# Switched attention: the pair products of two tiles in one matmul, in odd slots

## The chip, the cores and the metric

The kernel runs on one core of a Trainium2 chip. The metric is the time of one execution of the whole program in microseconds (us), taken on the device; lower is better. The figures for the kernel before come from three runs and from one profiled execution.

## The reference

The reference is a decoder of four blocks over x of 128 x 64 x 128 floats. Each block adds an attention and a feed-forward part. The change touches only the last part, a switched attention over 8 heads with 8 experts each, of which 2 are chosen for each token and head:

```python
gate_v = _get_sel_gate(x, sel_v_w, rs)      # sigmoid of the logits, top 2 of 8, normalised
gate_o = _get_sel_gate(x, sel_o_w, rs)
q = jnp.einsum('bsd,hpd->bhsp', x, q_w.reshape(H, P, D))
k = jnp.einsum('bsd,hpd->bhsp', x, k_w.reshape(H, P, D))
xv = jnp.einsum('bsd,hedp->bshep', x, v_w.reshape(H, E, D, P))
v = jnp.einsum('bshep,bshe->bhsp', xv, gate_v)
att = jax.nn.softmax(jnp.einsum('bhqp,bhkp->bhqk', q, k) * SCALE, axis=-1)
ctx = jnp.einsum('bhqk,bhkp->bqhp', att, v)
weighted = ctx[:, :, :, None, :] * gate_o[..., None]
out = jnp.einsum('bshep,hepd->bsd', weighted, o_w.reshape(H, E, P, D))
```

Its input is the layer norm of x, and its result is added to x times a gate.

## The kernel before

The last part is `switch_attention` (L1731 on). The other parts come before it and end at about 1211 us of the profiled span. Work is cut into 64 tiles of 128 tokens (two sequences of 64). `straight` (L36) writes each engine's program: for slot t = 0, 1, 2 ... it goes through that engine's list of stages `(lag, step)` and calls `step(t - lag)`. So a slot holds steps of several tiles, the order inside it is the order of the list, and every engine works through its own list strictly in order. Semaphores (`q[...]`) join the engines.

What a slot holds on each engine:

- TensorE: 16 units (`unit`, L2202 on), v0 to v7 of one tile and o0 to o7 of the tile before it. A unit is six 128x512 matmuls at L2221 on numbers split in a high and a low part: three fill bank `ps_a` (experts 4 to 7), three fill bank `ps_d` (experts 0 to 3). There are two banks of each, so unit n waits until unit n-2 has been read. Between the units stand small fp32 products: `turn_x` (L2229), `turn_probs` (L2236, two halves), `logits` (L2243), `pair_keys` (L2254), `scores` (L2278) and `context` (L2267).
- `pair_keys` multiplies the turned x of a tile with a 128x128 matrix per head, W["pair"] (key weights times query weights, made once), and so gives u; `scores` multiplies u with x. It is done in two halves of four heads, in banks `ps_w[0]` and `ps_w[1]`; `context` writes the same two banks.
- ScalarE scales `ps_a` with the gates (L1962, four instructions for a unit), and copies x, u (`keep_u`, L1993), the turned probabilities and the context out of PSUM; `exp_logits` (L1985) starts the routing of a tile.
- VectorE mixes `ps_d` into the sums (L2117, four instructions for a unit). Between these halves of units stand the 20 steps R0 to R19 of `route` (L2126 to L2147), which need `exp_logits`. They begin after the first half of v3, and a table, `between`, gives each its place.
- GpSimd adds the parts up: `add_v` (L1889, L1894) for each v unit, `add_o` for each o unit, `finish` for the output.

`context` of a tile stands on TensorE behind o1 and waits for v of all eight heads:

```python
wait_alone(pe, (q["v"], SH * i + SH), (q["p_kept"], i + 1), (q["uT"], 2 * upto))
```

The lags before are 1 for turn_x, pair_keys, logits, scores and routing, 2 for the v units, the turned probabilities and context, and 3 for the o units. The weights are loaded and split in a high and a low part once: V in slot 1, O in slots 2 and 3 (16 halves, between the v units' steps on ScalarE, L2023, and on VectorE, L2063).

Of the kernel before, what the change touches and what calls it, by code (L numbers as in the profile page):

```python
# [1730 lines left out]
def switch_attention(k, A, C, x_in, out):  # L1731
# [6 lines left out]
    with k.scope():  # L1738
# [31 lines left out]
        place = k.sb("sw_place", [P, 2 * SH, SE])  # L1770
# [3 lines left out]
        r = {n: k.sb("sw_r_" + n, G) for n in ("plus", "p", "eq1", "w1", "sel1", "p2", "eq2", "w2", "sel2", "sel")}  # L1774
# [47 lines left out]

        with nc.Block() as block:
            @block.sync
            def _(sp):
# [5 lines left out]
                sp.dma_start(place[:], A["c_place"].rearrange("p (g e) -> p g e", e=SE)).then_inc(q["place"], 16)  # L1831
# [203 lines left out]
            def _(dve):  # L2035
# [85 lines left out]
                def route(n):  # L2121


                    def step(i, s, rd):
                        ops = [
                            lambda: dve.tensor_scalar(r["plus"][:], decays[:], 1.0, None, ALU.add),  # L2126
                            lambda: dve.reciprocal(r["p"][:], r["plus"][:]),
                            lambda: dve.tensor_reduce(rm["m1"][:], r["p"][:], AX.X, ALU.max),
                            lambda: dve.tensor_tensor(r["eq1"][:], r["p"][:], wide(rm["m1"][:]), ALU.is_equal),
                            lambda: dve.tensor_tensor(r["w1"][:], r["eq1"][:], place[:], ALU.mult),  # L2130
                            lambda: dve.tensor_reduce(rm["w1"][:], r["w1"][:], AX.X, ALU.max),
                            lambda: dve.tensor_tensor(r["sel1"][:], r["w1"][:], wide(rm["w1"][:]), ALU.is_equal),
                            lambda: dve.scalar_tensor_tensor(out=r["p2"][:], in0=r["sel1"][:], scalar=-2.0, in1=r["p"][:],
                                                             op0=ALU.mult, op1=ALU.add),
                            lambda: dve.tensor_reduce(rm["m2"][:], r["p2"][:], AX.X, ALU.max),
                            lambda: dve.tensor_tensor(r["eq2"][:], r["p2"][:], wide(rm["m2"][:]), ALU.is_equal),
                            lambda: dve.tensor_tensor(r["w2"][:], r["eq2"][:], place[:], ALU.mult),
                            lambda: dve.tensor_reduce(rm["w2"][:], r["w2"][:], AX.X, ALU.max),
                            lambda: dve.tensor_tensor(r["sel2"][:], r["w2"][:], wide(rm["w2"][:]), ALU.is_equal),
                            lambda: dve.tensor_tensor(r["sel"][:], r["sel1"][:], r["sel2"][:], ALU.add),  # L2140
                            lambda: dve.tensor_tensor(chosen[:, s], r["p"][:], r["sel"][:], ALU.mult),
# [245 lines left out]
```

## Time and profile before

| | us |
|---|---|
| median of three runs | 3170.46 |
| lowest, highest | 3169.66, 3173.8 |
| profiled execution, its own time | 3168.74 |
| its span in the trace | 3167.0 |
| TensorE busy | 2907.0 (92%) |
| VectorE busy | 2780.7 (88%) |
| ScalarE busy | 2341.8 (74%) |
| GpSimd busy | 2322.8 (73%) |

The profiled execution is 1.7 us under the median, and its span is 1.7 us under its own time. Busy shares are means over all parts. In the timeline a row gives the start, the time from the first start to the last end, the engine, the line, and what it writes from what; times in square brackets are idle time before it and what ended it. Matmuls overlap in the pipeline, so the distance from start to start tells what one costs the engine, not its length. An fp32 matmul leaves two records, so "x8" at L2254 is four matmuls.

### The profile page before, as it was taken

To read this page: it belongs to the slowest core of one execution; us is meant where nothing else is said; L and a number is where in the kernel's file an instruction comes from. 1 tells how busy PE (TensorE), PEld (TensorE's weight loads), DVE (VectorE), ACT (ScalarE), POOL (GpSimd) and SP (SyncE) were. 2 spreads that over 40 slices of the span, in tenths; PEclk is the share of its full clock that TensorE was granted. 3 is DMA by queue.
4 is the path that set the end of the run, shared out by engine and by line. 5 is a ranking of instruction groups with operands and counts; after the bars stand their busy time and mean duration, and the time that the engine had idled before them with its cause. 6 is when DMAs were issued, how large, how long until landed. Compare 5 with 4: busy or idle time off the path is not lost.

```text
span 3167.0 us, 78218 instructions
## 1 busy us (share of the span) xinstructions
PE 2907.0 (92%) x24620; PEld 2176.0 (69%) x24620; DVE 2780.7 (88%) x9085; ACT 2341.8 (74%) x7546; POOL 2322.8 (73%) x3112
## 2 busy tenths in 40 slices
PE   7489992897689996999999999999999999999998
PEld 7257762675357774677777777777777777777776
DVE  6789997899989986888888888898898898898897
ACT  4866668888976665777777777777777777777776
POOL 2799994666876662677777777777777777777777
PEclk8589995898789997999999999999999999999999
DMA  4000000220000004100000000000000000000000
GB/s 131 8 2 2 2 2 18 68 75 13 1 6 16 16 16 109 30 9 8 7 9 8 7 9 8 7 9 8 7 9 8 8 9 8 7 9 8 7 8 6
DMA packets 114508, 55.31 MB, mean 17 GB/s; under 512 B 18352, under 2 KB 113712, under 8 KB 114096
## 3 DMA queue, kind: packets, MB, share of 16 engines
q1 hardware_dynamic: 114096, 50.30, 5.8%
q8 instruction: 200, 3.28, 0.4%
q14 instruction: 212, 1.74, 0.2%
HBM read 41.81 MB, written 8.45 MB: 16 GB/s over the span
## 4 chain that ended last, share of the span: by engine, by line
PE 59%; DVE 1%; ACT 1%; POOL 1%; DMA 0%; issue 0%; SPq 0%; POOLq 0%; ACTq 0%; DVEq 0%
PE ps_sw_a L2221 24%; PE ps_sw_d L2221 22%; PE ps_sw_w L2267 4%; PE ps_sw_w L2254 3%; PE ps_sw_s L2236 2%; PE ps_sw_s L2278 2%; PE ps_sw_m L2243 1%; ACT sw_scaled L1962 0%; DVE sw_v_part L2117 0%; PE ps_sw_m L2229 0%; DMA sw_v<-in_L_ffn_v_w 0%; POOL sw_v_pair L1889 0%; DVE sw_v_low L2056 0%; DVE sw_o_low L2063 0%; ACT sw_v_high L2017 0%
## 5 line engine op out<-in xcount | busy, mean ns | idle before, releaser
L1962 ACT ACTIVATE sw_scaled<-ps_sw_a,sw_gate_o 128x128 f32<-128x128 f32 x2048 | 620.3, 447 | 254.1 <-PE ps_sw_a L2221 247.0
L1962 ACT ACTIVATE sw_scaled<-ps_sw_a,sw_gate_v 128x128 f32<-128x128 f32 x2048 | 597.3, 448 | 196.2 <-PE ps_sw_a L2221 194.4
L2117 DVE SCALAR_TENSOR_TENSOR sw_o_part<-ps_sw_d,sw_gate_o,sw_o_part 128x128 f32<-128x128 f32 x1920 | 555.6, 339 | 63.1 <-PE ps_sw_d L2221 60.5
L1889 POOL TENSOR_TENSOR sw_v_pair<-sw_v_part,sw_scaled 128x256 f32<-128x256 f32 x512 | 381.9, 746 | 157.0 <-DVE sw_v_part L2117 91.6
L2117 DVE SCALAR_TENSOR_TENSOR sw_v_part<-ps_sw_d,sw_gate_v,sw_scaled 128x128 f32<-128x128 f32 x1024 | 303.9, 337 | 126.1 <-PE ps_sw_d L2221 107.1
L1915 POOL TENSOR_TENSOR sw_o_rest<-sw_o_rest,sw_scaled 128x256 f32<-128x256 f32 x384 | 285.4, 743 | 158.0 <-ACT sw_scaled L1962 120.7
L2117 DVE SCALAR_TENSOR_TENSOR sw_v_part<-ps_sw_d,sw_gate_v,sw_v_part 128x128 f32<-128x128 f32 x1024 | 304.8, 339 | 0.0
L1918 POOL TENSOR_TENSOR sw_o_rest<-sw_o_rest,sw_scaled 128x256 f32<-128x256 f32 x384 | 282.6, 736 | 30.1
L1894 POOL TENSOR_TENSOR sw_v<-sw_v_pair 128x128 f32<-128x128 f32 x512 | 244.6, 478 | 40.1
L1014 POOL TENSOR_TENSOR at_key_wide<-at_keyT,c_half_heads 128x1024 f32<-128x1024 f32 x128 | 242.6, 1895 | 4.6 <-ACT at_keyT L1112 4.6
L2221 PE MATMUL ps_sw_a<-sw_v_high,sw_xT_high 128*128 128x512 f32 x512 | 234.5, 458 | 8.2 <-DVE sw_v_low L2056 8.2
L2221 PE MATMUL ps_sw_a<-sw_o_high,sw_ctx_high 128*128 128x512 f32 x512 | 215.7, 421 | 0.2 <-ACT sw_scaled L1962 0.2
L2221 PE MATMUL ps_sw_d<-sw_v_high,sw_xT_high 128*128 128x512 f32 x512 | 207.6, 405 | 0.3 <-DVE sw_v_part L2117 0.3
L2221 PE MATMUL ps_sw_d<-sw_o_high,sw_ctx_high 128*128 128x512 f32 x512 | 202.1, 395 | 1.2 <-DVE sw_v_part L2117 1.2
L2221 PE MATMUL ps_sw_d<-sw_o_low,sw_ctx_high 128*128 128x512 f32 x512 | 202.7, 396 | 0.0
L2221 PE MATMUL ps_sw_a<-sw_o_high,sw_ctx_low 128*128 128x512 f32 x512 | 202.7, 396 | 0.0
L2221 PE MATMUL ps_sw_a<-sw_v_high,sw_xT_low 128*128 128x512 f32 x512 | 202.5, 396 | 0.0
L2221 PE MATMUL ps_sw_a<-sw_v_low,sw_xT_high 128*128 128x512 f32 x512 | 202.2, 395 | 0.0
L2221 PE MATMUL ps_sw_d<-sw_o_high,sw_ctx_low 128*128 128x512 f32 x512 | 202.1, 395 | 0.0
L2221 PE MATMUL ps_sw_a<-sw_o_low,sw_ctx_high 128*128 128x512 f32 x512 | 202.1, 395 | 0.0
L2221 PE MATMUL ps_sw_d<-sw_v_high,sw_xT_low 128*128 128x512 f32 x512 | 201.8, 394 | 0.0
L2221 PE MATMUL ps_sw_d<-sw_v_low,sw_xT_high 128*128 128x512 f32 x512 | 200.7, 392 | 0.0
(337 smaller groups left out, 8511.3 us busy)
## 6 DMA issues: line engine op xcount, KB each, us to landing
re_values<-in_ctx SPq DMA_DIRECT2D x128, 64.0 KB, 2.4
l_ctx<-in_ctx SPq DMA_DIRECT2D x16, 256.0 KB, 4.5
x<-in_x SPq DMA_DIRECT2D x16, 256.0 KB, 4.6
re_ctx<-in_ctx SPq DMA_DIRECT2D x16, 256.0 KB, 3.1
scratch_x<-x SPq DMA_DIRECT2D x64, 64.0 KB, 1.5
sw_x<-scratch_x SPq DMA_DIRECT2D x64, 64.0 KB, 1.9
sw_x_res<-scratch_x SPq DMA_DIRECT2D x64, 64.0 KB, 1.8
out<-sw_y SPq DMA_DIRECT2D x64, 64.0 KB, 1.5
```

Source lines behind the costliest of these rows:

```text
L1014: pool.tensor_tensor(key_wide[:, s], keyT[:, s].unsqueeze(1).broadcast_to([P, HALF, P]), C["half_heads"][:].unsqueeze(2).broadcast_to([P, ...
L1889: pool.tensor_tensor(v_pair[:, h % 2], v_part[:, h], scaled[:, h % 4, 2:4], ALU.add)\
L1894: pool.tensor_tensor(v[:, h], v_pair[:, h % 2, 0], v_pair[:, h % 2, 1], ALU.add).then_inc(q["v"], 1)
L1915: pool.tensor_tensor(o_rest[:, 0:2], o_rest[:, 0:2], scaled[:, h % 4, 0:2], ALU.add)\
L1918: pool.tensor_tensor(o_rest[:, 2:4], o_rest[:, 2:4], scaled[:, h % 4, 2:4], ALU.add)\
L1962: act.activation(scaled[:, h % 4, e], ps_a[h % 2][:, e], ACT.Copy, scale=gates[:, s, h, HALF_E + e:HALF_E + e + 1]).then_inc(a_scaled[kind ...
L2117: dve.scalar_tensor_tensor(out=acc[:, e % 2], in0=ps_d[h % 2][:, e], scalar=gates[:, s, h, e:e + 1], in1=before, op0=ALU.mult, op1=ALU.add ...
L2221: m = pe.matmul(bank, lhs[a], w[b][:, h, experts], start=c == 0, stop=c == 2)
L2236: m = pe.matmul(ps_s[t, h], probs[t, s, h], C["ident"][t, t], start=True, stop=True)
L2254: m = pe.matmul(ps_w[n][:, h * P:(h + 1) * P], W["pair"][:, 4 * n + h], xT[:, s], start=True, stop=True)
L2267: m = pe.matmul(ps_w[b][:, h * S:(h + 1) * S], v[t, h], probs_T[t, h], start=True, stop=True)
L2278: m = pe.matmul(ps_s[t], xT[:, s, t], uT[:, :, t], start=True, stop=True)
```

## The change

Pair products are made for two tiles at once. x of four tiles is kept (`xT` has four places), u for two (`uT` [P, SH, 2, P]). `pair_keys` runs only for even tiles and multiplies each pair matrix with the 256 columns of x of tiles i and i+1. Its eight matmuls for a pair of tiles (before: sixteen of 128 columns) stand in two blocks of four: the first directly behind the first half of the turned probabilities, the second between v4 and v5. With the new lag of 3 they all fall in odd slots. The lags are now 1 for turn_x, 3 for pair_keys, logits, scores, routing and the rounded x, 4 for v, turned probabilities and context, 5 for o, 6 for the store. The preparation of the weights keeps its lags 1 to 3. ScalarE's rounded x is made from `xT` in SBUF, behind the second unit, and a pair has four `keep_u` copies as before, now all in one slot, two of them ahead of `exp_logits`. To make room the routing works in place: three tiles in the place of ten, and one row of `place` read by all groups.

```diff
-        xT = k.sb("sw_xT", [P, 2, P])
+        xT = k.sb("sw_xT", [P, 4, P])
...
-        uT = k.sb("sw_uT", [P, SH, P])
+        uT = k.sb("sw_uT", [P, SH, 2, P])
...
-        r = {n: k.sb("sw_r_" + n, G) for n in ("plus", "p", "eq1", "w1", "sel1", "p2", "eq2", "w2", "sel2", "sel")}
+        r = {n: k.sb("sw_r_" + n, G) for n in ("equal", "sel", "p2")}
...
+        def of_pair(step):
+            def at(i, s, rd):
+                if i % 2 == 0:
+                    step(i, s, rd)
+            return at
...
-                    act.activation(xT[:, s], ps_m[:, 0], ACT.Copy).then_inc(q["xT"], 1)
-                    act.activation(xT_high[:, s], ps_m[:, 0], ACT.Copy).then_inc(q["xT_high"], 1)
+                    act.activation(xT_high[:, s], xT[:, i % 4], ACT.Copy).then_inc(q["xT_high"], 1)
...
-                        act.activation(uT[:, 4 * n:4 * n + 4], ps_w[n].rearrange("p (h t) -> p h t", h=4), ACT.Copy)\
-                            .then_inc(q["uT"], 1)
-                    return step
+                        act.activation(uT[:, 2 * n:2 * n + 2], ps_w[n % 2].rearrange("p (h c t) -> p h c t", h=2, c=2),
+                                       ACT.Copy).then_inc(q["uT"], 1)
+                    return of_pair(step)
...
-                stages = vs[:2] + [(1, keep_x)] + vs[2:4] + [(1, exp_logits), (2, keep_probs)] + vs[4:6]
-                stages += [(1, keep_u(0)), vs[6], (1, keep_u(1)), vs[7]] + os[:3] + [(2, keep_ctx(0)), os[3], exps[0]]
...
+                stages = vs[:2] + [(1, keep_x), (3, round_x), vs[2], (3, keep_u(0)), vs[3], (3, keep_u(1)), (3, exp_logits), (4, keep_probs)]
+                stages += [vs[4], vs[5], (3, keep_u(2)), vs[6], (3, keep_u(3)), vs[7]] + os[:3]
...
+                            both = xT[:, i % 4:i % 4 + 2].rearrange("p c t -> p (c t)")
+                            for h in range(2):
+                                m = pe.matmul(ps_w[n % 2][:, 2 * h * P:2 * (h + 1) * P], W["pair"][:, 2 * n + h], both,
+                                              start=True, stop=True)
+                            m.then_inc(q["u"], 1)
+                    return of_pair(step)
...
-                    wait_alone(pe, (q["v"], SH * i + SH), (q["p_kept"], i + 1), (q["uT"], 2 * upto))
-                    if isinstance(i, int) and i == TILES - 1:
+                    wait_alone(pe, (q["v"], SH * i + SH), (q["p_kept"], i + 1))
+                    if i % 2 and i < TILES - 1:
+                        pe.wait_ge(q["uT"], 2 * (i + 3))
+                    elif i:
                         pe.wait_ge(q["ctx_low"], 2 * i)
...
-                stages = vs[:2] + [(1, turn_x), turns[0], vs[2], turns[1], (1, logits), vs[3], vs[4], (1, pair_keys(0))]
-                stages += [vs[5], (1, pair_keys(1)), vs[6], vs[7], os[0], (1, scores), os[1], (2, context)]
-                stages += os[2:]
+                turns = [(4, lambda i, s, rd, lo=lo: turn_probs(i, s, rd, lo)) for lo in (0, 4)]
+                stages = vs[:2] + [(1, turn_x), turns[0], (3, pair_keys(0)), vs[2], turns[1], (3, logits), vs[3], vs[4], (3, pair_keys(2))]
+                stages += vs[5:] + [os[0], (3, scores), os[1], (4, context)] + os[2:]
```

TensorE from the turned x behind v1 to the first product of v2, before, in every slot:

```order
L2229 MATMUL ps_sw_m<-c_ident,sw_xhat 128x128
L2236 MATMUL ps_sw_s<-c_ident,sw_probs 64x64 x8
L2221 MATMUL ps_sw_a<-sw_v_high,sw_xT_high 128x512
L2221 MATMUL ps_sw_a<-sw_v_low,sw_xT_high 128x512
L2221 MATMUL ps_sw_a<-sw_v_high,sw_xT_low 128x512
```

The same place now, in an odd slot:

```order
L2243 MATMUL ps_sw_m<-c_ident,sw_xhat 128x128
L2250 MATMUL ps_sw_s<-c_ident,sw_probs 64x64 x8
L2272 MATMUL ps_sw_w<-sw_xT,sw_pair 128x256 x4
L2233 MATMUL ps_sw_a<-sw_v_high,sw_xT_high 128x512
L2233 MATMUL ps_sw_a<-sw_v_low,sw_xT_high 128x512
L2233 MATMUL ps_sw_a<-sw_v_high,sw_xT_low 128x512
```

Four matmuls of 256 columns have come in ahead of v2; an even slot has none there. A second place, TensorE from the end of v4 on, before, in every slot (`sw_w<-sw_xT,sw_pair` is pair_keys):

```order
L2221 MATMUL ps_sw_d<-sw_v_high,sw_xT_low 128x512
L2254 MATMUL ps_sw_w<-sw_xT,sw_pair 128x128 x4
L2221 MATMUL ps_sw_a<-sw_v_high,sw_xT_high 128x512
L2221 MATMUL ps_sw_a<-sw_v_low,sw_xT_high 128x512
L2221 MATMUL ps_sw_a<-sw_v_high,sw_xT_low 128x512
L2221 MATMUL ps_sw_d<-sw_v_high,sw_xT_high 128x512
L2221 MATMUL ps_sw_d<-sw_v_low,sw_xT_high 128x512
L2221 MATMUL ps_sw_d<-sw_v_high,sw_xT_low 128x512
L2254 MATMUL ps_sw_w<-sw_xT,sw_pair 128x128 x4
```

Now, in an odd slot, one block is left there, of 256 columns, and none stands between v5 and v6; in an even slot both are gone. ScalarE around `exp_logits` (`sw_exp`), before, in every slot:

```order
L1962 ACTIVATE sw_scaled<-ps_sw_a,sw_gate_v 128x128 x8
L1985 ACTIVATE sw_exp<-ps_sw_m 128x128
L1979 ACTIVATE sw_probs_T<-ps_sw_s 128x512
L1962 ACTIVATE sw_scaled<-ps_sw_a,sw_gate_v 128x128 x8
L1993 ACTIVATE sw_uT<-ps_sw_w 128x512
```

And now, in an odd slot, from v2 on:

```order
L1968 ACTIVATE sw_scaled<-ps_sw_a,sw_gate_v 128x128 x4
L2004 ACTIVATE sw_uT<-ps_sw_w 128x512
L1968 ACTIVATE sw_scaled<-ps_sw_a,sw_gate_v 128x128 x4
L2004 ACTIVATE sw_uT<-ps_sw_w 128x512
L1996 ACTIVATE sw_exp<-ps_sw_m 128x128
L1990 ACTIVATE sw_probs_T<-ps_sw_s 128x512
L1968 ACTIVATE sw_scaled<-ps_sw_a,sw_gate_v 128x128 x8
L2004 ACTIVATE sw_uT<-ps_sw_w 128x512
```

Two copies of u have moved ahead of `exp_logits`, one of them between the scaling of v3 and it. VectorE's order inside a slot is as before.

## Rows read from the trace of the kernel before

**Rows 1.** The page's first part: busy time, share of the span, instructions.
```profile
PE 2907.0 (92%) x24620; PEld 2176.0 (69%) x24620; DVE 2780.7 (88%) x9085; ACT 2341.8 (74%) x7546; POOL 2322.8 (73%) x3112
```
**Rows 2.** Busy time by stretches: span, PE, PEld, DVE, ACT, POOL, clock, DMA, GB/s.
```profile
2000.00:2200.00 200.00, 199.90 (x1225) 153.21 (x1223) 180.26 (x646) 152.13 (x595) 151.64 (x235) 1.00 0.03 8
```
**Rows 3.** Timeline of TensorE, context of two tiles, 29 slots apart.
```profile
1329.52 2.00 PE L2267 MATMUL ps_sw_w<-sw_probs_T,sw_v 64*128 64x64 f32 x32
...
2188.78 2.00 PE L2267 MATMUL ps_sw_w<-sw_probs_T,sw_v 64*128 64x64 f32 x32
```
**Rows 4.** Timeline of TensorE in one slot, from v0 to context.
```profile
2051.24 0.47 PE L2221 MATMUL ps_sw_a<-sw_v_high,sw_xT_high 128*128 128x512 f32 x1
...
2058.76 0.39 PE L2221 MATMUL ps_sw_d<-sw_v_high,sw_xT_low 128*128 128x512 f32 x1
...
2060.15 0.39 PE L2221 MATMUL ps_sw_d<-sw_v_high,sw_xT_low 128*128 128x512 f32 x1
2060.38 1.05 PE L2254 MATMUL ps_sw_w<-sw_xT,sw_pair 128*128 128x128 f32 x8
2061.18 0.48 PE L2221 MATMUL ps_sw_a<-sw_v_high,sw_xT_high 128*128 128x512 f32 x1
2061.49 0.40 PE L2221 MATMUL ps_sw_a<-sw_v_low,sw_xT_high 128*128 128x512 f32 x1
...
2067.77 1.08 PE L2278 MATMUL ps_sw_s<-sw_uT,sw_xT 128*64 128x512 f32 x4
2068.78 0.50 PE L2221 MATMUL ps_sw_a<-sw_o_high,sw_ctx_high 128*128 128x512 f32 x1
...
2070.37 2.00 PE L2267 MATMUL ps_sw_w<-sw_probs_T,sw_v 64*128 64x64 f32 x32
```
**Rows 5.** Timeline of VectorE in the same slot.
```profile
2059.23 0.61 DVE L2117 SCALAR_TENSOR_TENSOR sw_v_part<-ps_sw_d,sw_gate_v,sw_scaled 128x128 f32<-128x128 f32 x2 [1.17 <-PE ps_sw_d L2221]
2059.84 0.23 DVE L2126 TENSOR_SCALAR sw_r_plus<-sw_exp 128x128 f32<-128x128 f32 x1
...
2064.47 0.81 DVE L2132 TENSOR_TENSOR sw_r_sel<-sw_r_w,sw_m_w 128x128 f32<-128x128 f32 x1
...
2066.75 0.81 DVE L2136 TENSOR_TENSOR sw_r_eq<-sw_r_p,sw_m_m 128x128 f32<-128x128 f32 x1
...
2068.20 0.60 DVE L2117 SCALAR_TENSOR_TENSOR sw_v_part<-ps_sw_d,sw_gate_v,sw_v_part 128x128 f32<-128x128 f32 x2
...
2074.01 0.61 DVE L2117 SCALAR_TENSOR_TENSOR sw_o_part<-ps_sw_d,sw_gate_o,sw_o_part 128x128 f32<-128x128 f32 x2 [0.89 <-PE ps_sw_d L2221]
```
**Rows 6.** Timeline of GpSimd in the same slot: parts of v6 and v7.
```profile
2066.66 0.74 POOL L1889 TENSOR_TENSOR sw_v_pair<-sw_v_part,sw_scaled 128x256 f32<-128x256 f32 x1 [0.99 <-ACT sw_scaled L1962]
...
2068.94 0.74 POOL L1889 TENSOR_TENSOR sw_v_pair<-sw_v_part,sw_scaled 128x256 f32<-128x256 f32 x1 [1.00 <-DVE sw_v_part L2117]
2069.76 0.46 POOL L1894 TENSOR_TENSOR sw_v<-sw_v_pair 128x128 f32<-128x128 f32 x1
```
**Rows 7.** Timeline of ScalarE in the same slot, behind the scaling of v3.
```profile
2059.51 0.30 ACT L1985 ACTIVATE sw_exp<-ps_sw_m 128x128 f32<-128x128 f32 x1
2059.67 0.63 ACT L1979 ACTIVATE sw_probs_T<-ps_sw_s 128x512 f32<-128x512 f32 x1
2060.15 1.18 ACT L1962 ACTIVATE sw_scaled<-ps_sw_a,sw_gate_v 128x128 f32<-128x128 f32 x4
```
**Rows 8.** Start of the part: ScalarE's V halves, VectorE's O half, the first context.
```profile
1236.00 2.04 ACT L2017 ACTIVATE sw_v_high<-sw_v_part 128x1024 fp32r<-128x1024 f32 x2
...
1251.71 0.68 DVE L2063 TENSOR_TENSOR sw_o_low<-sw_o_part,sw_o_high 128x512 fp32r<-128x512 f32 x1
...
1272.22 3.68 PE L2267 MATMUL ps_sw_w<-sw_probs_T,sw_v 64*128 64x64 f32 x32 [5.86 <-POOL sw_v L1894]
```
**Rows 9.** DMA issues from 1200 to 1320 us: count, KB, us to landing.
```profile
sw_o_part<-in_L_ffn_o_w SPq DMA_DIRECT2D x4, 256.0 KB, 3.8
```
**Rows 10.** VectorE at the start of the part, GpSimd idle.
```profile
1229.53 0.29 DVE L2132 TENSOR_TENSOR sw_r_sel<-sw_r_w,sw_m_w 128x128 f32<-128x128 f32 x1
```

More of the change, by code:

```diff
@@ L1830, in _ @@
                 sp.dma_start(route_scale[:], on_all(A["L3_ffn_route_scale"], 1)).then_inc(prep["small"], 16)
[L1831 removed]
+                sp.dma_start(place[:], A["c_place"][:, 0:SE]).then_inc(q["place"], 16)
                 def tile_in(dst, i):
@@ L2124, in step @@
                     def step(i, s, rd):
+                        p = decays
                         ops = [
[L2126 to L2130, printed above, removed]
@@ L2131, in step @@
-                            lambda: dve.tensor_reduce(rm["w1"][:], r["w1"][:], AX.X, ALU.max),
-                            lambda: dve.tensor_tensor(r["sel1"][:], r["w1"][:], wide(rm["w1"][:]), ALU.is_equal),
-                            lambda: dve.scalar_tensor_tensor(out=r["p2"][:], in0=r["sel1"][:], scalar=-2.0, in1=r["p"][:],
+                            lambda: dve.tensor_scalar(p[:], decays[:], 1.0, None, ALU.add),
+                            lambda: dve.reciprocal(p[:], p[:]),
+                            lambda: dve.tensor_reduce(rm["m1"][:], p[:], AX.X, ALU.max),
@@ new lines, in step @@
+                            lambda: dve.tensor_tensor(r["equal"][:], p[:], wide(rm["m1"][:]), ALU.is_equal),
+                            lambda: dve.tensor_tensor(r["equal"][:], r["equal"][:], place[:].unsqueeze(1).broadcast_to(G), ALU.mult),
+                            lambda: dve.tensor_reduce(rm["w1"][:], r["equal"][:], AX.X, ALU.max),
+                            lambda: dve.tensor_tensor(r["sel"][:], r["equal"][:], wide(rm["w1"][:]), ALU.is_equal),
+                            lambda: dve.scalar_tensor_tensor(out=r["p2"][:], in0=r["sel"][:], scalar=-2.0, in1=p[:],
@@ L2140, in step @@
-                            lambda: dve.tensor_tensor(r["sel"][:], r["sel1"][:], r["sel2"][:], ALU.add),
-                            lambda: dve.tensor_tensor(chosen[:, s], r["p"][:], r["sel"][:], ALU.mult),
+                            lambda: dve.tensor_tensor(r["equal"][:], r["p2"][:], wide(rm["m2"][:]), ALU.is_equal),
+                            lambda: dve.tensor_tensor(r["equal"][:], r["equal"][:], place[:].unsqueeze(1).broadcast_to(G), ALU.mult),
+                            lambda: dve.tensor_reduce(rm["w2"][:], r["equal"][:], AX.X, ALU.max),
@@ L2241, in logits, with pair_keys @@
                         pe.wait_ge(prep["kept"], 1)
-                    pe.wait_ge(q["xT_high"], i + 1)
-                    pe.matmul(ps_m[:, 1], xT[:, s], W["sel"][:], start=True, stop=True).then_inc(q["logits"], 1)
-                def pair_keys(n):
+                    pe.wait_ge(q["xT"], min(i + 3, TILES))
+                    pe.matmul(ps_m[:, 1], xT[:, i % 4], W["sel"][:], start=True, stop=True).then_inc(q["logits"], 1)
+                def pair_keys(lo):
                     def step(i, s, rd):
-                        if i == 0:
-                            pe.wait_ge(prep["kept"], 2 + n)
-                        elif not first(i, 2):
-                            pe.wait_ge(q["ctx_low"], 2 * (i - 2) + n + 1)
-                        else:
-                            pe.wait_ge(q["uT"], 1 + n)
-                        for h in range(4):
-                            m = pe.matmul(ps_w[n][:, h * P:(h + 1) * P], W["pair"][:, 4 * n + h], xT[:, s],
-                                          start=True, stop=True)
-                        m.then_inc(q["u"], 1)
-                    return step
+                        if lo == 0:
+                            pe.wait_ge(q["xT"], i + 2)
+                        for n in (lo, lo + 1):
+                            if n >= 2:
+                                pe.wait_ge(q["uT"], 2 * i + n - 1)
+                            elif i == 0:
+                                pe.wait_ge(prep["kept"], 3)
+                            else:
+                                pe.wait_ge(q["ctx_low"], 2 * (i - 2) + n + 1)
+                            both = xT[:, i % 4:i % 4 + 2].rearrange("p c t -> p (c t)")
[4 more added lines that the diff above has]
+                    return of_pair(step)
@@ L2271, in scores @@
                 def scores(i, s, rd):
-                    waits = [(q["uT"], 2 * i + 2)]
+                    waits = [(q["uT"], 4 * (i // 2) + 4)]
                     if not first(i, 1):
@@ L2277, in scores @@
                         t = slice(b * S, (b + 1) * S)
-                        m = pe.matmul(ps_s[t], xT[:, s, t], uT[:, :, t], start=True, stop=True)
+                        m = pe.matmul(ps_s[t], xT[:, i % 4, t], uT[:, :, s, t], start=True, stop=True)
                     m.then_inc(q["scores"], 1)
```

58 lines of the change are left out of this document (32 added, 26 removed).

## Prediction

> **What bounds the kernel now.** I read the busy shares first: TensorE 92% over the whole, VectorE 88% [rows 1]. In a steady stretch of the last part TensorE is busy without a gap (199.90 of 200 us) at a granted clock of 1.00, and VectorE stands at 180.26, 90% [rows 2]. That looks like a kernel bound by TensorE alone. Then the regularity: 29 slots take 2188.78 - 1329.52 = 859.26 us, 29.63 us each [rows 3]. So one slot can stand for all, and what is left is to ask how much slack the other engines have in it.
>
> For that I follow one slot from engine to engine. TensorE's last product of v3 starts at 2058.76 and lasts 0.39 [rows 4]. VectorE has waited 1.17 us for it and starts on v3 at 2059.23 [rows 5]. From there it has no idle time until behind v7: its next wait, 0.89 us, is the one at 2074.01. It ends v7 at about 2068.8. GpSimd takes v7 at 2068.94 and ends at 2069.76 + 0.46 = 2070.22 [rows 6]. TensorE starts context at 2070.37 [rows 4]. So there are two ways from v3 to context, TensorE's own products (11.6 us from 2058.76) and the way over VectorE's v3 to v7 and GpSimd, and they end within 0.15 us of each other. Some of that is the time from a signal to a start; I take the slack as 0.10. **This is the fact that decides**: from v3 to context TensorE can get faster by 0.1 us and no more, whatever is taken out of it. From context round to v3 of the next slot it is the other way round: VectorE waits for TensorE (0.89 us at the first o unit behind context, 1.17 at v3), so each us added to TensorE there is added to the slot.
>
> **The change part by part.**
>
> *Pair products, price.* A block of four (eight records) of 128 columns goes from 2060.38 to 2061.18, 0.80 us, and the product behind it takes 0.31 to the next start where 0.23 is normal (2060.15 to 2060.38) [rows 4]: 0.88 in all, 3.52 for a pair of tiles. The new block has eight records of 256 columns. Below, a record can't be cheaper than one of half the columns: 0.80 / 8 = 0.10, 0.88 for the block. Above, it can't be dearer than one of 512 columns, 1.01 / 4 = 0.25 at the scores, 2.0 for the block. Half of a 512-column record is 0.125, barely over the 0.10 that a 128-column record with its weights takes, so I take 0.12, with 0.04 for a weight load that nothing hides: 1.0 us a block, 2.0 for a pair. TensorE saves 1.5 us per pair of tiles.
>
> At the scores an fp32 matmul of 512 columns takes 0.505 us (1.01 for two) [rows 4]. The Trainium skill, "FP8 and Floating Point Precision", section "TensorE Precision Notes", says that true fp32 takes four passes through the array; at 2.4 GHz (granted clock 1.00) that would be 0.85 us for 512 columns, an estimate from that page, and a new block would be 1.7 us, which would make the sum 21 us longer. The trace disagrees, and its number is used.
>
> *Where they stand.* Both old blocks stood between v4 and v6, on the stretch with 0.1 us of slack. An even slot loses both, 1.76 us, and can use 0.1: TensorE will wait ahead of o0's second bank and at context instead. Even slot: 29.63 - 0.10 = 29.53. An odd slot has one block between v4 and v5 (TensorE's way there is 11.6 - 1.76 + 1.0 = 10.8 us, still shorter than the other), and one ahead of v2, on the stretch where VectorE waits for TensorE: +1.0 in full.
>
> *Copies ahead of exp_logits.* exp_logits starts at 2059.51 and ends at 2059.81, and VectorE's R0 starts at 2059.84, in the middle of its gapless run [rows 5, 7]. In an odd slot a copy of 128x512 now stands between the scaling of v3 and exp_logits. Such a copy holds ScalarE for 2060.15 - 2059.67 = 0.48 us [rows 7]. R0 and all behind it start 0.48 later: +0.48. The bounds are 0 (if ScalarE has it behind it in time) and 0.6. The first of these copies, ahead of v3, is hidden: there TensorE's product of v3 is what ScalarE waits for, as VectorE does. The copies behind v5 and v6 stand as before. Keeping x before rounding it, the rounding from SBUF and the longer lags add nothing to either way in a steady slot: what they feed is wanted a slot later.
>
> *Routing in place.* The same 20 operations with the same shapes, in the same places on VectorE, each waiting for the one before as now: 0, bounds -0.2 and +0.2 per slot.
>
> *Odd slot*: 29.53 + 1.0 + 0.48 = 31.01. A pair of slots is 60.54 against 59.26: +1.28.
>
> *The two more slots at the start.* V's preparation was queued on ScalarE behind tile 0's softmax and starts at 1236.00 [rows 8]; now tile 0's softmax is in slot 3, and V can start up to 10 us earlier. But all 16 halves of O now stand ahead of v0 of tile 0, where half of them lay between its units. A round of four buffers is a landing of 3.8 us [rows 9], a rounding of about 0.65, a subtraction of 0.68 [rows 8] and an issue, 5.5 us, so four rounds take 22: V ready at about 1239, the first four halves half loaded by then, O at about 1257, the softmax at 1259. A slot takes 2070.37 - 2051.24 = 19.1 us from v0 to context [rows 4], so the first context comes at 1278 (now 1272.22), the second, behind 2 us of context, in an odd slot, at 1300.5, the third 29.5 later, at 1330. It is at 1329.52 now [rows 3]. Fill: +0.5, bounds -8 and +12. The end has the same steps, shifted by two slots: 0.
>
> *Sum.* Odd slots from 7 to 65 are 30: 30 x 1.28 = 38.4, and 0.5: +39. On the profiled execution's 3168.74 us that is 3207.6. The median of the runs is 1.7 higher than that execution, so I forecast **3208 us**, between the two.
>
> **The rivals.**
>
> *Slower, but by more.* A record of 256 columns costs near 0.25, so a block 2.0. Only the block ahead of v2 counts, the other has 1.2 us of room: +1.0 per pair, 3238. Against: half of the 512-column record. Chance 0.08.
>
> *Nothing that can be told.* A single VectorE wait of 0.5 us goes in every slot and the late exp_logits is hidden: a pair is 29.03 + 30.03 = 59.06, -6 us. Within 0.2% (6 us, about what a measurement of this kernel can tell from no change): 0.05.
>
> *Faster, TensorE alone decides.* If the other way had slack that I don't see, the whole 1.52 us per pair would be gained, 31 times, 47 us: 3122. For it: the gapless TensorE [rows 2]. It decides from 1.7 us of slack per slot on; I read 0.1. Chance 0.08.
>
> *Faster, VectorE's run shortens.* Two of its operations take 0.81 us (at 2064.47 and 2066.75), and the second starts within 0.1 us of GpSimd's part of v6 at 2066.66 and ends with it [rows 5, 6]; the same operation with GpSimd idle took 0.29 [rows 10]. If the moved work parts them, the run is 1.0 us shorter, a slot 28.53, an odd one 30.01, a pair 58.54: -0.72, 3147. It decides from 0.65 us per slot on. Against: GpSimd starts there because VectorE has just ended the unit, so the two stay tied in every slot. Chance 0.09. The Trainium skill, "SBUF — State Buffer", section "SBUF: two separate sides", gives this mechanism: the two share a port pair that one of them holds for a whole instruction. The trace agrees.
>
> **How the numbers follow.** My forecast, with its own range 3190 to 3222 (fill -8 to +12, exp_logits from 0 to 0.6), has 0.70; the rivals 0.08, 0.05, 0.08, 0.09. Slower by over 0.2%: 0.78; same 0.05; faster 0.17. The range leaves out the two faster cases (0.17) and the far end of the dear block: 3178 to 3230.
>
> **What would show it.** Right: context to context alternates, near 29.5 and 31.0; in TensorE's timeline the product ahead of o0's second bank and context wait 1.5 us in even slots, ended by VectorE and GpSimd; the block ahead of v2 takes about 1.0; VectorE's wait for v2 or v3 is 1 us longer in odd slots, and a wait of 0.5 us for ScalarE appears ahead of R0; VectorE's time at L2117 is as before. Wrong: slots that alternate near 28 and 30 with TensorE still gapless (TensorE alone), operations of 0.81 fallen to 0.3 (the shorter run), or a first context later than 1290 (fill).

## The result and the profile after

The changed kernel takes 3256.1 us (median of four runs, 3251.69 to 3257.53), the kernel before 3171.94 in the same session. The ratio is 1.0263, 95% interval 1.0246 to 1.0281: 84 us slower. The forecast had the sign and the alternating slots, but only 39 us more, and its range ended at 3230. The profiled execution took 3255.74, with a span of 3254.0 against 3167.0: 87.0 us to explain.

First the page's first part of the changed kernel (busy time, share of the span, instructions), then its busy time by stretches from 2000 to 2200 us (span, PE, PEld, DVE, ACT, POOL, clock, DMA, GB/s).

```profile
PE 2935.1 (90%) x24095; PEld 2145.2 (66%) x24108; DVE 2785.9 (86%) x9085; ACT 2345.3 (72%) x7546; POOL 2314.1 (71%) x3112
```

```profile
2000.00:2200.00 200.00, 195.73 (x1140) 144.21 (x1138) 172.72 (x618) 148.16 (x582) 149.48 (x232) 1.00 0.03 8
```

Every engine is as busy in total as before, within 1% [rows 1], and all are idler in the steady stretch [rows 2]: TensorE has lost 4 us of 200 to waits where it had no gap, at the same granted clock. TensorE issues 512 records fewer (24108, as the weight loads count; 13 matmul records are missing from this trace) and is busy 28 us longer. Now TensorE's timeline, context of tiles 2 and 62 and of three tiles between them:

```profile
1341.61 2.00 PE L2288 MATMUL ps_sw_w<-sw_probs_T,sw_v 64*128 64x64 f32 x32
...
2021.07 2.00 PE L2288 MATMUL ps_sw_w<-sw_probs_T,sw_v 64*128 64x64 f32 x32
...
2053.24 2.00 PE L2288 MATMUL ps_sw_w<-sw_probs_T,sw_v 64*128 64x64 f32 x32
...
2082.80 2.00 PE L2288 MATMUL ps_sw_w<-sw_probs_T,sw_v 64*128 64x64 f32 x32
...
3194.02 2.00 PE L2288 MATMUL ps_sw_w<-sw_probs_T,sw_v 64*128 64x64 f32 x32
```

Slots alternate: 32.17 us (odd) and 29.56 (even), where each took 29.63 [rows 3]. From tile 2 to tile 62 it is 1852.41 us; before, with the contexts at 1329.52 and 3107.06, 1777.54: 74.9 more. From the last of these to the end it is 59.98 against 59.94. The rest, 12.1, lies ahead of tile 2's context: 2.2 of it before the part begins (VectorE's first instruction of the part is at 1216.67 against 1214.49; the change touches nothing there, and over the profiled executions of this document that start scatters from 1211.63 to 1218.85), 9.9 in the part's start.

The two blocks of one odd slot, TensorE's timeline (start, length, engine, line, output and inputs):

```profile
2034.82 0.68 PE L2250 MATMUL ps_sw_s<-c_ident,sw_probs 64*64 64x64 f32 x16
2035.43 1.99 PE L2272 MATMUL ps_sw_w<-sw_xT,sw_pair 128*128 128x256 f32 x8
2037.08 0.58 PE L2233 MATMUL ps_sw_a<-sw_v_high,sw_xT_high 128*128 128x512 f32 x1
2037.49 0.39 PE L2233 MATMUL ps_sw_a<-sw_v_low,sw_xT_high 128*128 128x512 f32 x1
...
2042.43 1.89 PE L2272 MATMUL ps_sw_w<-sw_xT,sw_pair 128*128 128x256 f32 x8
2043.97 0.58 PE L2233 MATMUL ps_sw_a<-sw_v_high,sw_xT_high 128*128 128x512 f32 x1
2044.38 0.40 PE L2233 MATMUL ps_sw_a<-sw_v_low,sw_xT_high 128*128 128x512 f32 x1
```

From start to start the first block costs 2037.08 - 2035.43 = 1.65, and the product behind it 0.41 where 0.23 is normal: 1.83 us. The second costs 1.54 and 0.18, 1.72. Together 3.55 for a pair of tiles, against 3.52 for the four old blocks [rows 4]. **Joining the products saved TensorE nothing**: 256 columns cost twice what 128 do. The forecast had 1.0.

VectorE in the same slot; in square brackets the idle time ahead of a row and what ended it:

```profile
2038.88 0.61 DVE L2128 SCALAR_TENSOR_TENSOR sw_v_part<-ps_sw_d,sw_gate_v,sw_scaled 128x128 f32<-128x128 f32 x2 [2.04 <-PE ps_sw_d L2233]
...
2041.30 0.61 DVE L2128 SCALAR_TENSOR_TENSOR sw_v_part<-ps_sw_d,sw_gate_v,sw_scaled 128x128 f32<-128x128 f32 x2 [0.72 <-PE ps_sw_d L2233]
2042.40 0.23 DVE L2138 TENSOR_SCALAR sw_exp<-sw_exp 128x128 f32<-128x128 f32 x1 [0.49 <-ACT sw_exp L1996]
...
2045.78 0.61 DVE L2128 SCALAR_TENSOR_TENSOR sw_v_part<-ps_sw_d,sw_gate_v,sw_scaled 128x128 f32<-128x128 f32 x2 [0.44 <-PE ps_sw_d L2233]
...
2047.46 0.81 DVE L2144 TENSOR_TENSOR sw_r_sel<-sw_r_equal,sw_m_w 128x128 f32<-128x128 f32 x1
```

The first row is v2: VectorE waits 2.04 for the block ahead of it, where it waited 0.58 before. The wait of 0.49 for ScalarE ahead of R0 is there, as forecast. The fourth row is not in the forecast: VectorE waits again at v5, for TensorE, whose second block stands ahead of v5. v5 starts 4.48 us behind v3, and before it was 3.68 (2062.91, below, against 2059.23 [rows 5]). The 0.81-us operation is unchanged, so the rival of VectorE's shorter run is out. The same two rows, v2 and v5, before:

```profile
2056.80 0.61 DVE L2117 SCALAR_TENSOR_TENSOR sw_v_part<-ps_sw_d,sw_gate_v,sw_scaled 128x128 f32<-128x128 f32 x2 [0.58 <-PE ps_sw_d L2221]
...
2062.91 0.60 DVE L2117 SCALAR_TENSOR_TENSOR sw_v_part<-ps_sw_d,sw_gate_v,sw_scaled 128x128 f32<-128x128 f32 x2
```

Last TensorE's waits in an odd and the next even slot, at o0's second bank, and between them GpSimd's last v of the odd slot. It ends at 2052.73 + 0.46 = 2053.19, and context starts at 2053.24:

```profile
2049.55 0.50 PE L2233 MATMUL ps_sw_d<-sw_o_high,sw_ctx_high 128*128 128x512 f32 x1 [0.43 <-DVE sw_v_part L2128]
```

```profile
2052.73 0.46 POOL L1900 TENSOR_TENSOR sw_v<-sw_v_pair 128x128 f32<-128x128 f32 x1
```

```profile
2079.10 0.50 PE L2233 MATMUL ps_sw_d<-sw_o_high,sw_ctx_high 128*128 128x512 f32 x1 [0.59 <-DVE sw_v_part L2128]
```

So in both kinds of slot the way over VectorE and GpSimd now sets the end of the stretch from v3 to context. An odd slot is 29.56 + 1.83 ahead of v2 + 0.80 at v5 = 32.19, against 32.17 seen.

### The profile page after: what moved, and what is told of

It is laid out like the page before. It is cut to its first block, busy times and chain, and to the rows that moved or that the text cites. A ratio compares the mean times of both kernels' runs of the same rounds, so it can differ in the third digit from the quotient of the medians.

```text
span 3254.0 us, 77178 instructions
## 1 busy us (share of the span) xinstructions
PE 2935.1 (90%) x24095; PEld 2145.2 (66%) x24108; DVE 2785.9 (86%) x9085; ACT 2345.3 (72%) x7546; POOL 2314.1 (71%) x3112
## 4 chain that ended last, share of the span: by engine, by line
PE 47%; DVE 7%; ACT 4%; issue 3%; POOL 1%; DMA 1%; SPq 0%; DVEq 0%; ACTq 0%; POOLq 0%
PE ps_sw_a L2233 18%; PE ps_sw_d L2233 16%; DVE sw_v_part L2128 5%; PE ps_sw_w L2288 4%; ACT sw_scaled L1968 4%; PE ps_sw_w L2272 4%; PE ps_sw_s L2250 2%; PE ps_sw_s L2299 1%; PE ps_sw_m L2257 1%; DVE sw_r_equal L2142 0%; DVE sw_r_p L2145 0%; DMA sw_v<-in_L_ffn_v_w 0%; POOL sw_v_pair L1895 0%; DVE sw_m_w L2143 0%; PE ps_sw_m L2243 0%
## 5 line engine op out<-in xcount | busy, mean ns | idle before, releaser
L2233 PE MATMUL ps_sw_d<-sw_o_high,sw_ctx_high 128*128 128x512 f32 x512 | 208.8, 408 | 32.2 <-DVE sw_v_part L2128 32.2
```

The lines of the kernel that those rows point to most:

```text
L2233: m = pe.matmul(bank, lhs[a], w[b][:, h, experts], start=c == 0, stop=c == 2)
```

## The experiments

The theory behind them: taking TensorE work off the stretch from v3 to context gains 0.1 us of a slot at most, and work added anywhere costs what it takes. So the cost is the price of a block, weighed by its place. What was open was the price, why the row of the scores had misled, and what the late exponential and the start of the part are worth.

**Both blocks behind v4.**

```diff
-stages = vs[:2] + [(1, turn_x), turns[0], (3, pair_keys(0)), vs[2], turns[1], (3, logits), vs[3], vs[4], (3, pair_keys(2))]
-stages += vs[5:] + [os[0], (3, scores), os[1], (4, context)] + os[2:]
+stages = vs[:2] + [(1, turn_x), turns[0], vs[2], turns[1], (3, logits), vs[3], vs[4], (3, pair_keys(0)), vs[5], vs[6], (3, pair_keys(2))]
+stages += vs[7:] + [os[0], (3, scores), os[1], (4, context)] + os[2:]
...
```

ScalarE's list changes with it (not shown): all four copies of u stand behind v4, and `exp_logits` directly behind v3.

> The changed kernel (3256.1) with both blocks of pair products between v4 and v7 of odd slots, and ScalarE's copies behind them, so that exp_logits stands directly behind the scaling of v3 again. Theory A (from v3 to context TensorE has room for the two old blocks, 1.76 us, in every slot and no more; outside that stretch a block costs its whole price; a block of 256 columns is 1.83): even slots stay at 29.5; in odd slots TensorE's way from v3 to context is 11.6 - 1.76 + 3.66 = 13.5, 1.9 more than the other way, and nothing stands ahead of v2: 31.4 to 31.5. A pair 61.0 against 61.73, 20 us less, about 3236. Theory B (the dear part of the change is only the block ahead of v2 and the late exp_logits): odd 29.6, a pair 59.2, about 3180. Theory C (the place is of no account, the longer lags or the routing cost the time): within 6 us of 3256.

Measured: 3227.3 us (ratio to before 1.0174, 1.0159 to 1.0189), 29 less than the changed kernel. The contexts of an odd slot:

```profile
2009.71 2.00 PE L2288 MATMUL ps_sw_w<-sw_probs_T,sw_v 64*128 64x64 f32 x32
...
2040.95 2.00 PE L2288 MATMUL ps_sw_w<-sw_probs_T,sw_v 64*128 64x64 f32 x32
```

31.24, expected 31.4 to 31.5; even slots 29.51. The time was expected at 3236. A block behind v4 costs 1.72 and the two 3.44, 1.68 more than before, and 29.63 + 1.68 = 31.31. Theory A stands, with the price read a little too high, and theories B and C fall.

**Only 64 stationary columns.**

```diff
-m = pe.matmul(ps_w[n % 2][:, 2 * h * P:2 * (h + 1) * P], W["pair"][:, 2 * n + h], both,
+m = pe.matmul(ps_w[n % 2][0:S, 2 * h * P:2 * (h + 1) * P], W["pair"][:, 2 * n + h, 0:S], both,
```

> The changed kernel (3256.1) with only 64 of the 128 columns of each pair matrix as the stationary operand: the matmuls still have 256 moving columns, all copies and places are as in the changed kernel, and half of the key components is left out of the scores. Theory A (an fp32 product with 128 stationary columns takes twice the passes of one with 64, which is why the scores, with 64, told me too low a price): a record falls from 0.207 to about 0.11 us and a block from 1.83 to 0.9 to 1.0. The block ahead of v2 gives 0.9 back in every odd slot, and the one behind v4 whatever v5's wait for TensorE is, 0.3: odd 31.0, about 3256 - 36 = 3220 (3215 to 3228). Theory B (the price goes by moving columns alone): no record changes, within 6 us of 3256. Theory C (the slot waits for GpSimd and VectorE whatever TensorE does ahead of v2): records get shorter and the time stays at 3256.

Measured: 3266.9 (ratio 1.0300, 1.0285 to 1.0316), slower than the changed kernel. A block with its start and the product behind it:

```profile
2042.12 1.94 PE L2272 MATMUL ps_sw_w<-sw_xT,sw_pair 128*64 128x256 f32 x8
2043.99 0.50 PE L2233 MATMUL ps_sw_a<-sw_v_high,sw_xT_high 128*128 128x512 f32 x1
```

The block takes 1.87 us. **Theory A, as put here, is wrong**: fewer stationary columns make an fp32 product no cheaper.

**Two halves side by side.** What is left that sets the scores apart is their output: one of their two products writes partitions 0 to 63, the other 64 to 127.

```diff
-m = pe.matmul(ps_w[n % 2][:, 2 * h * P:2 * (h + 1) * P], W["pair"][:, 2 * n + h], both,
+m = pe.matmul(ps_w[n % 2][h * S:(h + 1) * S, 2 * h * P:2 * (h + 1) * P], W["pair"][:, 2 * n + h, 0:S], both,
```

> The narrow stationary operand alone made nothing cheaper (a block of four 64-column products still took 1.87 us, and the time was 3266.9), so theory A as put for it has fallen. New theory D: what makes the scores cheap (1.01 us for two products of 512 columns) is that the two write different halves of the partitions, 0 to 63 and 64 to 127, and so run side by side in two halves of TensorE's columns; each takes its full four passes. This run is the changed kernel with 64 of the 128 columns of each pair matrix, as in the narrow run, but the two products of one bank write different halves of the partitions (half of the key components is left out). D: a block falls from 1.87 to 0.9 to 1.0; that is the price that my prediction had, so it also tests the rest of its sum: odd slots 31.0, even 29.53, fill +12, 3171.9 + 38 + 12 = 3222 (3210 to 3228). Rival E (the shape of the moving operand, 512 columns in steps, is what makes the scores cheap): the block stays at 1.87 and the time at 3267.

```profile
2015.91 1.08 PE L2272 MATMUL ps_sw_w<-sw_xT,sw_pair 128*64 128x256 f32 x8
2016.93 0.50 PE L2233 MATMUL ps_sw_a<-sw_v_high,sw_xT_high 128*128 128x512 f32 x1
```

Measured: 3213.2 (ratio 1.0138, 1.0124 to 1.0152). The same eight records with the same operand shapes cost 1.02 instead of 1.87 by their place in the output alone. D stands and E falls. The contexts of an odd and an even slot:

```profile
2001.58 2.00 PE L2288 MATMUL ps_sw_w<-sw_probs_T,sw_v 64*128 64x64 f32 x32
...
2032.51 2.00 PE L2288 MATMUL ps_sw_w<-sw_probs_T,sw_v 64*128 64x64 f32 x32
...
2062.01 2.00 PE L2288 MATMUL ps_sw_w<-sw_probs_T,sw_v 64*128 64x64 f32 x32
```

With a block near the forecast's price, odd slots are 30.93 and even ones 29.50; the forecast had 31.01 and 29.53. Where the price is right, the rest of its sum for a steady slot holds.

**The scores written to one half.** The converse, on the kernel before. It leaves out the scores of the second sequence of each tile; four matmuls at the start (not shown) fill the bank once.

```diff
-m = pe.matmul(ps_s[t], xT[:, s, t], uT[:, :, t], start=True, stop=True)
+m = pe.matmul(ps_s[0:S], xT[:, s, t], uT[:, :, t], start=True, stop=True)
```

> The kernel before with both products of the scores written to partitions 0 to 63 (the scores of the second sequence of a tile are left out, those of the first are overwritten; four matmuls at the start fill the bank once). Theory D (side by side in two halves of the columns): written to one half they run one after the other, and scores take 1.75 to 1.9 us instead of 1.01. As the stretch from v3 to context has 0.1 of room, each slot gets 0.65 to 0.8 longer, 64 of them 42 to 51: 3214 to 3223. Rival E (an fp32 product of 512 columns takes 0.5 us by itself): the scores stay at 1.01 and the time at 3172.

```profile
2026.93 1.93 PE L2278 MATMUL ps_sw_s<-sw_uT,sw_xT 128*64 128x512 f32 x4
2028.79 0.50 PE L2221 MATMUL ps_sw_a<-sw_o_high,sw_ctx_high 128*128 128x512 f32 x1
...
2030.38 2.00 PE L2267 MATMUL ps_sw_w<-sw_probs_T,sw_v 64*128 64x64 f32 x32
...
2060.88 2.00 PE L2267 MATMUL ps_sw_w<-sw_probs_T,sw_v 64*128 64x64 f32 x32
```

Measured: 3220.0 (ratio 1.0157, 1.0143 to 1.0171). The scores take 1.86 us instead of 1.01 [rows 4], so one fp32 product of 512 columns takes 0.93, not the 0.505 that the forecast took. The slot is 30.50, 0.87 longer: on this stretch TensorE's added work has no room at all.

**exp_logits ahead of the second copy of u**, with the dear and with the cheap block (the same edit to the changed kernel and to the one with two halves):

```diff
-[..., (3, keep_u(0)), vs[3], (3, keep_u(1)), (3, exp_logits), (4, keep_probs)]
+[..., (3, keep_u(0)), vs[3], (3, exp_logits), (3, keep_u(1)), (4, keep_probs)]
```

> The changed kernel (3256.1) with exp_logits ahead of the second copy of u. Theory A (VectorE waits 0.49 for exp_logits at R0, but behind it v5 waits 0.44 for TensorE's second block, so the late exponential is hidden under that wait): the wait at R0 goes, the wait of v5's mixing grows from 0.44 to 0.9, no difference over 3 us. Theory B (the late exponential costs its 0.48 in every odd slot, as the prediction had it): 30 x 0.48 = 14 us less, 3242.

> The run with the pair products in two halves (half of the key components is left out), with exp_logits ahead of the second copy of u. With the dear block, exp_logits first gave 0.15 us in an odd slot (32.17 to 32.01). If D is right, TensorE's second block no longer delays v5, and the late exponential costs its whole 0.48: 30 x 0.48 = 14 us less than the run with exp_logits behind the copy, about 3207. Rival: it is hidden elsewhere, and the gain is 5 us or less, as with the dear block.

Measured: 3254.4 (ratio 1.0260, 1.0245 to 1.0275), odd slots 32.02, and v5's wait is 0.79: theory A. With the cheap block 3217.5 (ratio 1.0153, 1.0139 to 1.0167), odd slots 31.10 where they were 30.93: 4 us slower, and neither expectation holds. The intervals of the two times overlap, but from tile 2 to tile 62 the second profile is 6.2 us longer. VectorE's rows for v3 and v5 of an odd slot, first with two halves, then with the exponential first as well:

```profile
2021.09 0.61 DVE L2128 SCALAR_TENSOR_TENSOR sw_v_part<-ps_sw_d,sw_gate_v,sw_scaled 128x128 f32<-128x128 f32 x2 [0.76 <-PE ps_sw_d L2233]
2022.18 0.23 DVE L2138 TENSOR_SCALAR sw_exp<-sw_exp 128x128 f32<-128x128 f32 x1 [0.49 <-ACT sw_exp L1996]
...
2025.08 0.61 DVE L2128 SCALAR_TENSOR_TENSOR sw_v_part<-ps_sw_d,sw_gate_v,sw_scaled 128x128 f32<-128x128 f32 x2
2025.60 0.36 DVE L2142 TENSOR_TENSOR sw_r_equal<-sw_r_equal,sw_place 128x128 f32<-128x128 f32 x1
```

```profile
2022.71 0.61 DVE L2128 SCALAR_TENSOR_TENSOR sw_v_part<-ps_sw_d,sw_gate_v,sw_scaled 128x128 f32<-128x128 f32 x2 [0.73 <-PE ps_sw_d L2233]
...
2026.69 0.61 DVE L2128 SCALAR_TENSOR_TENSOR sw_v_part<-ps_sw_d,sw_gate_v,sw_scaled 128x128 f32<-128x128 f32 x2 [0.29 <-PE ps_sw_d L2233]
2027.22 0.56 DVE L2142 TENSOR_TENSOR sw_r_equal<-sw_r_equal,sw_place 128x128 f32<-128x128 f32 x1
```

With the exponential late there is a wait of 0.49 ahead of R0 and none at v5; with it early there is none at R0 and 0.29 at v5. v5 starts 3.99 and 3.98 behind v3 either way. So the late exponential and TensorE's block ahead of v5 are two ways to the same place, and the longer counts, not the sum. Behind v5 the second run is 0.2 longer at L2142 (0.56 against 0.36), which over 30 odd slots is 6 us. GpSimd's rows beside the two, first with two halves, then with the exponential first as well:

```profile
2025.07 0.74 POOL L1895 TENSOR_TENSOR sw_v_pair<-sw_v_part,sw_scaled 128x256 f32<-128x256 f32 x1 [0.73 <-ACT sw_scaled L1968]
```

```profile
2027.17 0.46 POOL L1900 TENSOR_TENSOR sw_v<-sw_v_pair 128x128 f32<-128x128 f32 x1
```

They end at 2025.81 and 2027.63, and VectorE's operation ends 0.15 us behind each (2025.96 and 2027.78), as its 0.81-us operation ends 0.16 behind GpSimd's [rows 5, 6]. So the length of L2142 goes with where GpSimd's work falls. That is read from the rows; no run moved GpSimd's work alone.

**Both: two halves, and both blocks behind v4**: the kernel of the first experiment with the edit of the third. Two of its added lines:

```diff
+stages = vs[:2] + [(1, turn_x), turns[0], vs[2], turns[1], (3, logits), vs[3], vs[4], (3, pair_keys(0)), vs[5], vs[6], (3, pair_keys(2))]
...
+m = pe.matmul(ps_w[n % 2][h * S:(h + 1) * S, 2 * h * P:2 * (h + 1) * P], W["pair"][:, 2 * n + h, 0:S], both,
```

> Both ideas together: the block at the price that my prediction had (two products side by side in two halves of the columns, 1.01 us; half of the key components is left out) and both blocks between v4 and v7 with exp_logits directly behind the scaling of v3. Theory (price times place): TensorE's way from v3 to context in odd slots is 11.6 - 1.76 + 2.03 = 11.9, 0.3 more than before and 0.4 over the other way; odd slots 29.9 to 30.1, even 29.5, a pair 59.4 to 59.6 against 59.26, 30 pairs +4 to +10, and the start +7 to +10: 3183 to 3190. Rival (joining the products for two tiles costs something beyond TensorE's time, by the copies of u or the waits of pairs): odd slots stay over 30.5 and the time over 3200.

Measured: 3194.5 (ratio 1.0074, 1.0057 to 1.0091), over the expectation's 3190. TensorE around the first block, and the contexts at the two ends of that odd slot:

```profile
2057.49 2.00 PE L2288 MATMUL ps_sw_w<-sw_probs_T,sw_v 64*128 64x64 f32 x32
...
2076.89 0.39 PE L2233 MATMUL ps_sw_d<-sw_v_high,sw_xT_low 128*128 128x512 f32 x1
2077.21 1.08 PE L2272 MATMUL ps_sw_w<-sw_xT,sw_pair 128*64 128x256 f32 x8
2078.23 0.50 PE L2233 MATMUL ps_sw_a<-sw_v_high,sw_xT_high 128*128 128x512 f32 x1
...
2087.81 2.00 PE L2288 MATMUL ps_sw_w<-sw_probs_T,sw_v 64*128 64x64 f32 x32
```

The product ahead of a block of this kind takes 0.32 to the next start and not 0.23, and the one behind it 0.34: a block is 1.02 + 0.09 + 0.11 = 1.22, two 2.44, 0.68 more than before. Odd slots are 2087.81 - 2057.49 = 30.32, 0.69 more. My 1.01 had left the neighbours out. In this profiled execution the rest is the start of the part, 7.2 longer than before up to tile 2's context.

**The lags alone**: the kernel before with the new lags, four places of x, two of u, x rounded from SBUF and the routing in place, but with products of 128 columns per tile at the old places:

```diff
-vs, os = ([(lag, unit(kind, h)) for h in range(SH)] for kind, lag in (("v", 2), ("o", 3)))
+vs, os = ([(lag, unit(kind, h)) for h in range(SH)] for kind, lag in (("v", 4), ("o", 5)))
...
-m = pe.matmul(ps_w[n][:, h * P:(h + 1) * P], W["pair"][:, 4 * n + h], xT[:, s],
+m = pe.matmul(ps_w[n][:, h * P:(h + 1) * P], W["pair"][:, 4 * n + h], xT[:, i % 4],
```

> The kernel before (3171.9) with all of the change but the joined products: lags 1/3/4/5/6, four places of x, two of u, rounded x from SBUF behind the second unit, routing in place; the pair products stay per tile, 128 columns, at the old places in every slot. Theory A (the steady slot pays only for the blocks, the two more slots at the start cost 12 us): slots of 29.63, first context at 1285, 12 us more, about 3184 (3178 to 3190). Theory B (the longer lags or the routing in place cost something in every slot): slots of over 29.8 and a time over 3195.

Measured: 3175.3 (ratio 1.0016, 1.0007 to 1.0026). Contexts of two neighbouring slots:

```profile
2016.59 2.00 PE L2280 MATMUL ps_sw_w<-sw_probs_T,sw_v 64*128 64x64 f32 x32
...
2046.22 2.00 PE L2280 MATMUL ps_sw_w<-sw_probs_T,sw_v 64*128 64x64 f32 x32
```

The slot is 29.63, and from tile 2 to tile 62 it is 1779.50 us against 1777.54: routing in place and the longer lags cost a steady slot 0.03 us at most, which is too little to tell from nothing. From VectorE's first instruction of the part to tile 2's context it is 1334.12 - 1213.94 = 120.2 against 115.0 before and 124.9 in the changed kernel. My 12 for the start was too much, and the time lies under the expected 3178 to 3190.

**O's preparation two slots later**:

```diff
-(2, only_first(fetch_o(4, 10))), (3, only_first(fetch_o(10, 16))), (6, store)])
+(4, only_first(fetch_o(4, 10))), (5, only_first(fetch_o(10, 16))), (6, store)])
...
-[st, (2, round_o(vs.index(st))), (3, round_o(SH + vs.index(st)))]
+[st, (4, round_o(vs.index(st))), (5, round_o(SH + vs.index(st)))]
...
-stages += [(2, low_o(n // 2)), (3, low_o(SH + n // 2))]
+stages += [(4, low_o(n // 2)), (5, low_o(SH + n // 2))]
```

> The changed kernel (3256.1) with O's loads and preparation two slots later (lags 4 and 5), so that they lie between the units of tiles 0 and 1 as before, not ahead of v0 of tile 0. From the start of the part (VectorE's first instruction in it) to the third context it is 115.0 us in the kernel before, 124.9 in the changed one and 120.2 with the lags alone. Theory (the halves of O ahead of v0 are what the longer lags cost): the third context comes 115 to 118 us after the start and the time falls by 7 to 10, about 3247. Rival (two more slots have to be passed by every engine, whatever is in them): 123 to 125 us and no difference over 3.

Measured: 3253.0 (ratio 1.0262, 1.0247 to 1.0277). That is the ratio of the changed kernel (1.0263), so the times show no gain. In the one profiled execution tile 2's context comes 121.4 behind the first instruction, 3.5 earlier, between the two expectations. How much of that is O is not settled: the run with `exp_logits` first, whose start differs in that order alone, has 127.7 where the changed kernel has 124.9.

**V rounded ahead of the exponentials**, on the kernel before, an attempt at a faster one:

```diff
-straight(stages + [(1, round_v(h)) for h in range(SH)])
+at = stages.index(exps[0])
+straight(stages[:at] + [(1, round_v(h)) for h in range(5)] + stages[at:] + [(1, round_v(h)) for h in range(5, SH)])
```

> The kernel before with five of V's eight roundings on ScalarE ahead of the exponentials of tile 0's softmax instead of behind them. At the start of the part VectorE waits 2.43 us for the first of them, then 0.66 and 2.20, and the last three loads wait for VectorE. If that queue is what sets the first context, it comes 2.4 to 5 us earlier and the time is 3167 to 3169.5. Rival: the exponentials, 2.3 us, or the landing of V set it, no difference.

Measured: 3169.7 against 3170.3 (ratio 0.9997, 0.9989 to 1.0006), no difference that can be told. In the profile tile 2's context comes 112.2 us behind the part's first instruction, 2.8 earlier than before (the first context was expected 2.4 to 5 earlier); the part itself began 2.2 later in that execution. A gain of this size can't be shown by these runs. No version here beats the kernel before.

## Why the prediction was right in sign and wrong in size

- *What bounds the kernel.* Right. Taking work off the stretch from v3 to context gave 0.07 us per even slot (29.56, forecast 29.53), though 1.76 us went. Adding there gave all of it (1.68 more gave 1.61, 0.85 more gave 0.87).
- *Pair products, price.* **This step failed.** I took an fp32 product of 512 columns at 0.505 us, half of the 1.01 of the scores, and so a record of 256 columns at 0.12. That row is two products that write different halves of the partitions and take their time together; written to one half they take 1.86. The upper bound of 2.0 held; the value taken, 1.0, was 1.83 and 1.72. TensorE saved nothing where 1.5 us per pair of tiles was reckoned. The better row stood in the same group: 0.88 for four products of 128 columns, twice that for 256. The Trainium skill, "FP8 and Floating Point Precision", section "TensorE Precision Notes", has four passes for true fp32; at 2.4 GHz (granted clock 1.00) that is an estimate of 0.43 us for 256 columns and of 0.85 for 512. I had set it aside as contradicted by the trace. The trace agrees within a tenth: 1.83 / 4 = 0.46, and 0.93 for 512. The Trainium skill, "TensorE: Matmul & The Clock Gate", section "Part 3: Packing small matmuls — row/col tiling", says that products which fill only a part of the array can run concurrently, and that the start partition of the output picks the columns of the array. The 1.86 against 1.01 agrees. The difference, 0.83 in each of 30 odd slots, is 25 us.
- *Where they stand.* Half right. The block ahead of v2 counted in full. The one behind v4 was given 1.2 of room, reckoned from v3 to context as a whole. But VectorE meets TensorE once more inside it, at v5, and v5 came 0.80 later. This too came with the price: with the cheap block, and the exponential as in the changed kernel, VectorE does not wait at v5, and the odd slot is 30.93 against the forecast's 31.01.
- *Copies ahead of exp_logits.* The wait of 0.49 appeared, and taking it away is worth 0.15 per odd slot in the changed kernel and nothing with the cheap block. A delay of 0.48 was forecast for this stretch and 0.80 came, by another way: 0.32 x 30 = 10 us.
- *Routing in place.* Right at 0 within 0.03 us per slot, by the run with the lags alone.
- *The start.* This step failed too: forecast +0.5 with a bound of +12, measured +12.1. The first three contexts were forecast at 1278, 1300.5 and 1330 and came at 1285.49, 1312.08 and 1341.61. So 7.5 were lost ahead of the first, 2.2 of them before the part begins, and 4.1 between the first and the second. The forecast had "V can start up to 10 us earlier", and it does (ScalarE's first half of V starts at 1227.75, before at 1236.00 [rows 8]), but tile 0's `exp_logits`, at 1256.23, now stands behind V and 12 of O's 16 halves. Against the run with the lags alone, which has 5.2 of the 9.9, the changed kernel loses 2.3 ahead of tile 0's context and 2.5 in the slot behind it (26.59 against 24.04), which is an odd one. What causes the 2.3, and what O's halves cost, stays open.
- *Sum.* The block ahead of v2 is 25 us over the forecast, the stretch from v3 to context 10, the start 11.6: 47, and 3208 + 47 = 3255, against 3256.1.

Of the rivals, the one with a dear block was nearest in mechanism (2.0 us, 3238), and it had a chance of 0.08. It too kept the second block free and the start at 0.5. With 1.83 and 0.80 in each odd slot and 12.1 at the start its sum gives about 3254.

## What to carry to other kernels

Before a row gives a price per column, see whether it is one product or several side by side: products that write different halves of the partitions shared their time here, and halving or doubling another row of the same kind tests that. Joining the moving operands of fp32 products, here from 128 to 256 columns, halved their number and not their time. Where two engines meet several times in a stretch, room must be counted to each meeting and not to the end; and two delays ahead of one meeting need not add.

## What was not expected of the hardware

- Two fp32 products of 64 stationary columns took little more than the time of one when they wrote partitions 0 to 63 and 64 to 127: 1.02 us for four of 256 columns, against 1.87 with all in one half, and 1.01 against 1.86 for two of 512.
- Four products with half as many stationary columns (1.87 and 0.11 behind them) cost more than with all 128 (1.65 and 0.18).
- Behind v4, the product ahead of a block with 64 stationary columns also takes 0.32 us to the next start where 0.23 is normal.
